# A two-layer fp32 transformer step: first layer begun by chunks, second layer's fold done by transposes and a VectorE sum

## The reference

```python
# layer 0, attention: 16 heads of 8, causal softmax, rms-norm and rope on q and k
qkv = LN(x) @ w_qkv.T;  q, k = rope(rms(q)), rope(rms(k))
x += softmax(causal(q @ k.T / sqrt(8))) @ v @ w_proj.T
# layer 0, mixer: a linear map given in the Fourier domain
x += real(ifft(fft(LN(x)) @ (w_freq_real + 1j * w_freq_imag))) + bias
# layer 1, linear attention: 16 heads of 8, elu + 1 features
x += ((Q @ (K.T @ V)) / (Q @ K.sum()) * sigmoid(stdp)) @ Wo.T + bo
# layer 1, attention over 8 heads of 64; each head's q, k, v is a gated sum of the
# top 3 of 5 experts (gates Ws for q, Wd for k and v), no causal mask;
# the output goes to the experts again by a 0/1 choice and through Wo
x += experts(softmax(q @ k.T / 8) @ v) @ Wo
```

## Time and profile before

| what | value |
|---|---|
| median of 3 runs | 1671.5 us (1671.23 to 1671.99) |
| the profiled execution, its own time | 1671.58 us |
| its span, first to last instruction | 1669.7 us |
| TensorE, VectorE busy | 1553.2 us (93%), 1244.7 us (75%) |
| ScalarE, GpSimd busy | 947.4 us (57%), 825.4 us (49%) |
| mean granted TensorE clock | 0.978 |

### The profile page before, as it was taken

The page is one execution under the profiler, slowest core; times in us unless marked ns, Lnnn a source line. Parts: engine busy times, 40 slices in busy tenths (PEclk is TensorE's granted clock), DMA queues, the critical chain, the costliest instruction groups (busy, mean ns, idle before and its releaser), DMA issues.

```text
span 1669.7 us, 27307 instructions
## 1 busy us (share of the span) xinstructions
PE 1553.2 (93%) x8490; PEld 1012.1 (61%) x8490; DVE 1244.7 (75%) x2525; ACT 947.4 (57%) x1590; POOL 825.4 (49%) x916
## 2 busy tenths in 40 slices
PE   3699999999899997679999999999999999999998
PEld 2455565565566556547667666567576676666565
DVE  3997687688588637787777778787778787777764
ACT  3446756755755662335655655655645656556653
POOL 2530000000001123468758879788689699698552
PEclk9799999999999999889999999999999999999999
DMA  2000000000000000000000000000000000000000
GB/s 64 0 1 1 2 1 1 1 1 1 1 1 1 1 13 12 1 1 13 1 13 1 1 13 1 1 13 1 13 1 1 13 1 1 1 1 1 1 7 20
DMA packets 12231, 9.41 MB, mean 6 GB/s; under 512 B 3840, under 2 KB 11584, under 8 KB 12096
## 3 DMA queue, kind: packets, MB, share of 16 engines
q1 hardware_dynamic: 12096, 7.66, 1.7%
HBM read 6.61 MB, written 1.05 MB: 5 GB/s over the span
## 4 chain that ended last, share of the span: by engine, by line
PE 63%; POOL 17%; DVE 11%; issue 4%; ACT 4%; SPq 1%; DMA 0%; DVEq 0%; ACTq 0%; POOLq 0%
PE ps L920 10%; PE ps L719 8%; PE ps L753 8%; PE ps L738 7%; PE ps L891 5%; PE ps L908 5%; PE ps L678 4%; PE ps L909 4%; POOL gs L1602 4%; POOL gsum L1603 3%; POOL z L583 3%; POOL onm L577 3%; PE ps L931 2%; DVE mxp L1269 2%; POOL h_qk L1604 2%
## 5 line engine op out<-in xcount | busy, mean ns | idle before, releaser
L1148 ACT ACTIVATE pbuf<-ps 128x512 f32<-128x512 f32 x512 | 301.7, 600 | 167.0 <-PE ps L909 163.3
L1013 ACT ACTIVATE pbuf<-ps 128x1024 f32<-128x1024 f32 (+3 forms) x320 | 280.5, 897 | 179.7 <-PE ps L741 91.5
L1269 DVE TENSOR_REDUCE mxp<-ps 128x1 f32<-128x512 f32 (+2 forms) x432 | 278.9, 685 | 88.9 <-PE ps L719 52.0
L1485 DVE TENSOR_TENSOR den<-den,pbuf 128x1024 f32<-128x1024 f32 x224 | 309.9, 1384 | 1.9
L920 PE MATMUL ps<-pbuf,h_v 128*64 128x512 f32 x1024 | 248.0, 605 | 0.0
L1134 ACT ACTIVATE relu<-ps 128x512 f32<-128x512 f32 x256 | 152.2, 598 | 160.2 <-PE ps L891 128.2
L1437 DVE TENSOR_TENSOR gt<-ps,gate 128x320 f32<-128x320 f32 x384 | 181.7, 484 | 77.5 <-POOL h_v L1612 38.8
L719 PE MATMUL ps<-kM,qT 128*128 128x512 f32 (+3 forms) x640 | 230.8, 412 | 8.7 <-ACT kM L1000 4.6
L908 PE MATMUL ps<-q1T,k1T 128*128 128x512 f32 x512 | 215.2, 420 | 10.3 <-ACT pbuf L1148 8.9
L1458 DVE CUSTOM_DVE_ANT_0 relu<-ps,relu 128x512 f32<-128x512 f32 x256 | 174.4, 684 | 67.3 <-PE ps L891 62.5
L738 PE MATMUL ps<-qT,kM 128*128 128x512 f32 (+3 forms) x640 | 202.0, 384 | 8.4 <-ACT pbuf L1013 8.3
(11 more groups left out here) (230 smaller groups left out, 2707.8 us busy)
## 6 DMA issues: line engine op xcount, KB each, us to landing
wraw<-in_Wkv SPq DMA_DIRECT2D x16, 160.0 KB, 2.6
wraw<-in_Wq SPq DMA_DIRECT2D x8, 160.0 KB, 2.2
out<-x SPq DMA_DIRECT2D x4, 256.0 KB, 2.3
wqkv<-in_wqkvT SPq DMA_DIRECT2D x1, 192.0 KB, 4.0
masks<-in_masks SPq DMA_DIRECT2D x1, 128.0 KB, 4.0
dft<-in_dft SPq DMA_DIRECT2D x1, 128.0 KB, 2.3
wout<-in_Wo SPq DMA_DIRECT2D x2, 64.0 KB, 2.6
ident<-in_ident SPq DMA_DIRECT2D x1, 64.0 KB, 5.8
```

What stands on the lines that cost most here:

```text
L1013: nc.scalar.activation(pbuf0[:, u % NP0, :, off:CH], ps[:, b:b + 2, off:CH], ACT.Exp, scale=float(D0) ** -0.5).then_inc(s_exp, 1)
L1148: nc.scalar.activation(pbuf1[:, u % NP1, i, :], ps[:, i, :], ACT.Exp, scale=float(D1) ** -0.5).then_inc(s_exp1, 1)
L1269: v.tensor_reduce(mxp[:, i, h:h + n, b], sc.rearrange("p (h k) -> p h k", h=n), AX.X, ALU.max).then_inc(s_read0d, 1)
L1485: v.tensor_tensor(dn, dn, w, ALU.add).then_inc(s_den1, 1)
```

## The change

1. **Loads.** `x` comes in four DMAs, one a chunk, with a semaphore each; `ident` after the first, `wqkv` after the second, each with its own semaphore. `fold` and its load go.
2. **Start by chunks.** Statistics, root, normalising, transposes, projections and evictions are interleaved by chunk; constants are prepared after the normalising.
3. **First four heads in two halves of 8 tiles.** Squares, roots, rotation and both stagings are done half by half, ahead of `SEQ0`; the first k and q steps wait for their half alone.
4. **Rest.** ScalarE squares the other twelve heads (two ACTIVATEs), GpSimd sums them by pairwise adds; VectorE keeps the reciprocals, now in chunk 1 of group 0. The Fourier matrices move into `SEQ0` (`fq`), the exponent of `stdp` too.
5. **Keeping TensorE at work.** 30 transposes without use ahead of `SEQ0` ("proj") and 40 within chunk 0 ("keys").
6. **Key copies.** Of `kM` for chunks 0 and 1 of groups 1 to 3, two of four copies go to VectorE (`K_BY_DVE`); the step k of chunk 1 comes behind q of chunk 0.
7. **Fold.** `F` is four transposes of `oT`, and VectorE adds the halves by a TENSOR_REDUCE from PSUM; a new step `den` with a bank of its own does the four matmuls for the sums, and VectorE takes the reciprocals and multiplies `on` in SBUF.
8. **q2 of layer 1.** `sq2` is fp32r, and four fp32r matmuls against `identr` replace the four fp32 transposes.

```diff
@@ preparation0
-        out += [(("stagek", g), 3), (("k", g, 0), 1), (("k", g, 1), 1)]
+        out += [(("stagek", g), 3), (("k", g, 0), 1)]
         if late:
             out.append((late, 1))
-        out += [(("stageq", g), 3), (("q", g, 0), 1)]
-        if g == 0:
-            out += [(("rest", 0), 1), (("rest", 1), 1)]
+        out += [(("stageq", g), 3), (("q", g, 0), 1), (("k", g, 1), 1)]
...
+            if (g, c) == (0, 0):
+                items.insert(2, (("fq", 0), 1))
+                items[3:3] = [(("keep", "keys"), 1), (("k", 0, 2), 1), (("rest", 0), 1)]
+                items.insert(9, (("fq", 1), 1))
+            if (g, c) == (0, 1):
+                items.insert(2, (("rest", 1), 1))
@@ foreground1
-                seq.append(("F", (u - 3) // M1 - 1))
+                seq += [("F", (u - 3) // M1 - 1), ("den", (u - 3) // M1 - 1)]
@@ sync
-            sp.dma_start(x[:], A["x"].rearrange("(n p) d -> p n d", p=P)).then_inc(s_load, 16)
+            for c in range(NC):
+                sp.dma_start(x[:, TPC * c:TPC * (c + 1), :], x_v[:, TPC * c:TPC * (c + 1), :]).then_inc(s_x[c], 16)
...
@@ tensor
+            pe.wait_ge(s_ident, 16)
+            transposes1(0)
+            pe.wait_ge(s_wqkv, 16)
+            for n in range(NT):
+                project(n)
+                if n % TPC == 1 and n // TPC + 1 < NC:
+                    transposes1(n // TPC + 1)
             pe.wait_ge(s_qkvev, NT)
             pe.wait_ge(s_const, 1)
...
+            keep_clock(ACC, "proj")
...
@@ q2 of layer 1
-                    chunk_transposes(ring1, step, lambda i: sq2[:, i, 0:D1 + 1], D1 + 1).then_inc(s_turn1, 1)
+                    for i in range(TPC):
+                        mm = pe.matmul(ps[0:D1 + 1, bank, P * i:P * (i + 1)], sq2[:, i, :], identr[:],
+                                       start=True, stop=True)
@@ F of layer 1, tensor
+                    for i in range(TPC):
+                        mm = pe.transpose(ps[:, bank, P * i:P * (i + 1)], oT[:, m % 2, P * i:P * (i + 1)], ident[:])
+                    mm.then_inc(s_turn1, 1)
+                elif kind == "den":
+                    m = step[1]
+                    bank = take(ring1, step)
                     pe.wait_ge(s_den1s, m + 1)
-                    for i in range(TPC):
-                        pe.matmul(ps[:, bank, D1 * i:D1 * (i + 1)], oT[:, m % 2, t], fold[:], ...
...
@@ scalar
+            for n in range(NT):
+                evict(n)
+                if n == 1:
+                    deviations(3)
+                if n % TPC == 1 and n // TPC + 1 < NC:
+                    tokens1(n // TPC + 1)
+                if n == 11:
+                    mean_squares(first, halves[0], 1)
+            act.wait_ge(s_qkvev, NT)
+            for i in range(2):
+                a, _, t, _, _, _ = heads(i, rest, slice(0, NT))
+                nc.scalar.activation(t, a, ACT.Square).then_inc(s_sqr, 1)
+            mean_squares(first, halves[1], 2)
...
-                        for h in range(GH):
+                        for h in range(2 if (g, c) in K_BY_DVE else GH):
@@ vector
+            for k, tiles in enumerate(halves):
+                dve.wait_ge(s_qkvev, NT // 2 * (k + 1))
+                squares(first, tiles)
+                link(roots(first, tiles, k + 1))
+                link(norm_and_rotate(v, link, first, tiles))
+                stage_keys(0, tiles)
+                stage_queries(0, tiles)
...
+                    for h in range(2, GH):
+                        rows = slice(32 * h, 32 * h + 32)
+                        ins = v.tensor_copy(kM[g % 2][rows, h, CH * c:CH * (c + 1)], ps[rows, ring0.bank(step), :])
...
-                    link(v.reciprocal(rd1[:], ps[:, b, TPC * D1:TPC * (D1 + 1)]))
-                    v.tensor_tensor(on[:], ps[:, b, 0:TPC * D1].rearrange("p (n d) -> p n d", n=TPC),
-                                    rd1[:].unsqueeze(2).to_broadcast([P, TPC, D1]), ALU.mult).then_inc(s_read1d, 1)
+                    o = ps[:, ring1.bank(step), :].rearrange("p (n a d) -> p n d a", n=TPC, a=2)
+                    v.tensor_reduce(on[:], o, AX.X, ALU.add).then_inc(s_read1d, 1)
+                elif kind == "den":
+                    m = step[1]
+                    wait_turn(dve, ring1, step)
+                    link(v.reciprocal(rd1[:], ps[:, ring1.bank(step), 0:TPC]))
+                    wait_read(dve, ring1, ("F", m))
+                    v.tensor_tensor(on[:], on[:], rd1[:].unsqueeze(2).to_broadcast([P, TPC, D1]),
+                                    ALU.mult).then_inc(s_read1d, 1)
@@ gpsimd
+            for i in range(2):
+                _, m, t, _, _, _ = heads(i, rest, slice(0, NT))
+                pool.wait_ge(s_sqr, i + 1)
+                link(g_.tensor_tensor(t[:, :, :, 0:4], t[:, :, :, 0:4], t[:, :, :, 4:8], ALU.add))
+                link(g_.tensor_tensor(t[:, :, :, 0:2], t[:, :, :, 0:2], t[:, :, :, 2:4], ALU.add))
+                g_.tensor_tensor(m.unsqueeze(3), t[:, :, :, 0:1], t[:, :, :, 1:2], ALU.add).then_inc(s_msr, 1)
```

More of the change, by code:

```diff
@@ L58 @@
 MAX1 = 2.0
[L59 removed]
+KEEP = {"proj": 30, "keys": 40, "pj": 28, "mix": 20, "lin": 14, "norm2": 8, "norm3": 6, "gates": 16, "end": 18}
 def preparation0():
@@ L179, in merge @@
     return seq
+K_BY_DVE = {(g, c): 2 * (g - 1) + c + 1 for g in range(1, NG) for c in range(2)}
 class Ring:
@@ L331, in build @@
         l1.close()
+        s_x = [sem(f"s_x{c}") for c in range(NC)]
+        s_ident = sem("s_ident")
+        s_sqr = sem("s_sqr")
+        s_msr = sem("s_msr")
+        s_kdve = sem("s_kdve")
+        s_wqkv = sem("s_wqkv")
         s_load = sem("s_load")
@@ L670, in take @@
                 if turn >= len(ring.banks):
-                    wait_read(pe, ring, ring.order[turn - len(ring.banks)])
+                    last = ring.order[turn - len(ring.banks)]
+                    if last[0] == "k":
+                        wait_keys(*last[1:])
+                    else:
+                        wait_read(pe, ring, last)
                 return ring.bank(step)
@@ L1196, in _, with centred @@
             v.memset(ones[:], 1.0)
-            dve.wait_ge(s_load, 16 * 12)
-            statistics(0, NT)
-            dve.wait_ge(s_std, 1)
-            link(v.reciprocal(rstd[:], std[:]))
-            norm(0, NT)
+            def centred(c):
+                tiles = slice(TPC * c, TPC * (c + 1))
+                dve.wait_ge(s_std, c + 1)
+                link(v.reciprocal(rstd[:, tiles], std[:, tiles]))
+                norm(TPC * c, TPC)
+            for c in range(NC):
+                dve.wait_ge(s_x[c], 16)
+                statistics(TPC * c, TPC)
+                if c:
+                    centred(c - 1)
+            centred(NC - 1)
+            dve.wait_ge(s_ident, 16)
+            dve.wait_ge(s_load, 16 * 9)
             v.tensor_copy(identr[:], ident[:])
@@ L1215, in squares @@
                 for i in range(2):
-                    _, m, t, _, _, _ = heads(i, hs)
+                    _, m, t, _, _, _ = heads(i, hs, tiles)
                     ins = v.tensor_reduce(m, t, AX.X, ALU.add)
                 ins.then_inc(s_ms, 1)
-            squares(first)
-            dve.wait_ge(s_rms, 1)
-            for i in range(2):
-                m = heads(i, first)[1]
-                ins = v.reciprocal(m, m)
-            link(ins)
-            link(norm_and_rotate(v, link, first))
@@ L1227, in _, with roots, stage_keys @@
-            dve.wait_ge(s_pconst, 1)
+            def roots(hs, tiles, count):
+                dve.wait_ge(s_rms, count)
+                for i in range(2):
+                    m = heads(i, hs, tiles)[1]
+                    ins = v.reciprocal(m, m)
+                return ins
+            def stage_keys(g, tiles):
+                gk = qkv[:, tiles, D + 32 * g:D + 32 * (g + 1)].rearrange("p n (h d) -> p n h d", d=D0)
+                v.tensor_copy(stagek[:, tiles, :, D0:2 * D0].bitcast(F32R), gk)
+                link(v.tensor_copy(stagek[:, tiles, :, 0:D0].bitcast(F32R), gk))
+                v.tensor_tensor(stagek[:, tiles, :, 2 * D0:3 * D0], gk, stagek[:, tiles, :, 0:D0],
+                                ALU.subtract).then_inc(s_stagek, 1)
```

222 lines of the change are left out of this document (115 added, 107 removed).

## The result

| | before | after |
|---|---|---|
| median, alternating on one chip | 1671.37 us (1669.78 to 1671.99, 4 runs) | 1650.84 us (1649.68 to 1651.37, 4 runs) |
| profiled span | 1669.7 us | 1649.5 us |
| mean granted clock | 0.978 | 0.984 |

The ratio is 0.9878, 95% interval 0.9861 to 0.9895: faster, but by 20.5 us where 45 were forecast, and outside the range of 1609 to 1645.

The account below looks back on a forecast made before the run. The prediction took TensorE, busy 93% of the span, as the main bound, though not everywhere, with GpSimd a third of layer 1's chain. Terms -18 - 14 - 13 = -45 from 1671.5 gave 1626.5 us, range 1609 to 1645.

Parts of the forecast that it names:

- Part 1: The beginning: earlier loads, chunked start and halved heads bring first exponents to about 55.5 us against 73.88, -18 us.
- GpSimd's sums of the other heads run beside it, for which I add 1: Beginning, staging of half 2: GpSimd's sums beside it add 1 us, so it ends at 35.5 instead of 34.5.
- The filling: Chunk 0 of the beginning: 40 idle TensorE transposes take 5.8 us from near 34.5; VectorE idles some 4 us.
- Part 2: Layer 0's three group boundaries: shared key copies nearly remove stalls and half-clock stretches, 4.7 us each, -14 us.
- Part 3: Layer 1's fold and q2: TensorE loses some 20 us of work, of which -13 us counts; bounds -3 and -21.
- two thirds realised: Layer 1: with a third of the chain GpSimd's, two thirds of TensorE's 20 us relief counts, -13 us.
- The 4 us put down for the multiplication beside GpSimd: Layer 1: VectorE's multiplication reading SBUF twice could make GpSimd stand, making the sum 4 us worse by the skill's rule.
- (a): Rival: layer 1 gives nothing, since GpSimd's chain takes back what TensorE is spared; 1639.5 us, chance 0.14.
- (b): Rival: the clock still falls at the group boundaries, as waits for staging remain; 1635.5 us, chance 0.12.
- (c): Rival: all of TensorE's relief counts; 1612.5 us, chance 0.13.
- (d): Rival: TensorE's clock falls once in each of layer 1's 32 chunks, +109 us; 1735.5 us, chance 0.03.
- (e): Rival: in the beginning, idle transposes and ScalarE's longer queue leave only 8 us of gain; 1636.5 us, chance 0.08.

Follow-up runs that it names:

- e3: Changed kernel with GpSimd's clearing of kM0 held back until the four chunks are normalised: 1647.55 us, ratio to before 0.9853.
- e4: Changed kernel with GpSimd's sums of the other twelve heads held back until both halves are staged: 1646.48 us, ratio to before 0.9840.
- e11: Changed kernel with kM0's clearing as GpSimd's first work, small clearings behind the normalising, sums held back, idle transposes kept: 1640.74 us, ratio to before 0.9821.
- e14: e12 with the other heads' root and stdp's exponent moved into chunk 1, VectorE's reciprocals eight steps later in chunk 1: 1637.91 us, ratio to before 0.9796.
- e12: e11 without the 40 idle transposes: 1639.12 us, ratio to before 0.9805; timed again 1640.86 us, ratio 0.9823.
- e5: Changed kernel without the 40 idle transposes of chunk 0: 1647.63 us, ratio to before 0.9850.
- e8: Kernel before with GpSimd's addition into z cut to 8 elements, leaving out most of that sum: 1657.54 us, ratio to before 0.9918.
- e9: Changed kernel with GpSimd's addition into z cut to 8 elements, leaving out most of that sum: 1628.78 us, ratio to before 0.9744.
- e1: Kernel before with only the new F, den step and q2 of layer 1: 1659.44 us beside 1672.01, ratio 0.9926.
- e13: e12 with the other heads' root and stdp's exponent moved into chunk 1, VectorE's reciprocals into chunk 2: 1641.71 us, ratio to before 0.9817.

## Why the prediction was wrong

**The step that failed is Part 1**: "normalised chunks at about 7.2, 9.8, 12.4 and 13.9 us", and behind it "GpSimd's sums of the other heads run beside it, for which I add 1". I took VectorE's durations from a stretch in which GpSimd was idle and moved them to one in which it isn't. The clearing of `kM0` at 4.43, 6.92 us long, is in the trace of before; I did not ask what runs beside the new place of the normalising. In a line:
```profile
4.43 6.92 POOL L1525 MEMSET kM<- 128x8192 f32 x1
```
The runs price the parts of the missing 17 to 18 us (first exponents at 73.1 for 55.5): the clearing 3.3 (e3), or 4.0 between e4 and e11; the sums 4.4 against the 1 I had put in (e4); and the work for the other heads ahead of the first exponents 5.6 to 7.0 there, of which 3.3 to 4.8 last (e14 against the two profiles of e12). I had named the reciprocals' move as a relief; they stood in chunk 1, but still ahead of the first exponents, and the root and the table load on ScalarE stood there too. This last price is the sum of two moves, which no run prices apart. Together this is 12 to 14 us more than I had put in. The filling's 4.5 (e5) is not among them: the 4 us in which VectorE idles were in my 55.5.

That e14 has its first exponents at 55.3 is therefore luck: it has no filling, and with it they would come near 59. Some 3 to 5 of the 18 us stay unexplained by the named causes. The milestones of e11, with both collisions gone and the filling kept, show where they build up: last eviction 24.9 (forecast 22.2), halves staged at 29.4 and 37.6 (26.2 and 35.5), third maximum 45.8 (41).

*The filling* was sized about right, 5.8 us long (measured 5.29) at a price of 4 (4.5), and put at 34.5 (48.53, as all before it was late). TensorE's stream in the changed kernel is nothing but idle transposes from 48.6 to 53.8, right behind the matmuls of `fq`; windows, columns as in the earlier trace rows:
```profile
49.00:50.00 1.00, 1.00 (x6) 1.00 (x5) 0.10 (x1) 0.37 (x1) 0.00 (x0) 0.50 0.00 0
...
51.00:52.00 1.00, 1.00 (x12) 1.00 (x10) 0.00 (x0) 0.00 (x0) 0.00 (x0) 1.00 0.00 0
...
58.00:60.00 2.00, 1.57 (x5) 1.02 (x5) 1.32 (x6) 1.36 (x3) 0.00 (x0) 0.50 0.00 0
```
The granted clock rose from 0.50 to 1.00 within them, and their starts went from 0.21 to 0.11 us apart. Here matmuls ran just before; in the kernel before TensorE had done nothing at all until its 16 transposes from 19.6 us on, and their starts too went from 0.21 us apart (the prediction has 0.19) to 0.11, at 23.07, still within them. The Trainium skill, "TensorE: Matmul & The Clock Gate", section "Part 4: PE-mode transpose", has it that transposes don't raise the clock; the measurement decides. But at 58 us the clock is at 0.50 again. From 54 to 68 us its mean is 0.86, against 0.51 in e5 without the filling, and e5 is ahead by 4.5 us at the first exponents all the same: the filling did keep the clock up for longer, and that was worth less than its length.

**Part 2** was right in mechanism and near in size: 10.8 us of 14, no 0.5 left at the boundaries, the pairs of copies as forecast, 3.6 a boundary instead of 4.7.

**Part 3** had TensorE's relief right (20; e8 and e9 give 19.4), and so the term that was off is "two thirds realised". It was 8.6, or 10.8 without the half-clock stretch, e1 gave 11.7: about half. A share of the chain is no exchange rate: GpSimd's 33% was not a third of each chunk's time but a second chain, which holds back one chunk of every four while the next head's projections run. Three gain 0.4 to 0.7 us and that one loses 0.35 to 0.5, about 0.3 a chunk on the mean; with GpSimd relieved it is 0.6 throughout. The 4 us put down for the multiplication beside GpSimd did not show: GpSimd's multiplications average 1030 ns in both kernels, and VectorE's takes 444 ns for 424.

**The rivals.** (a) named the right mechanism and overdid it: layer 1 gave 8.6, not 0. (b) fell: no profile with the shared copies has a half-clock stretch at a boundary. (c) holds only with GpSimd relieved (e9). (d) fell: one half-clock stretch in 885 us, not 32. (e), at 0.08, had the right place and was still 7 us too good, and its reason, idle transposes and ScalarE's longer queue, leaves out GpSimd's clearing and sums. Each term of the forecast came out smaller than its own value, which my range, built from one rival at a time, did not reach.

## What to carry to other kernels

Before a step of VectorE is moved, read GpSimd's row at its new place: there a duration taken from a quiet stretch need not hold, and even a clearing that reads nothing can stand in the way. When an engine that is no bottleneck lies to a third on the chain, relieve it in an experiment on both kernels: the difference shows what the change is worth without it. A gain in the first microseconds can be lost again where something moves with it: in e13 GpSimd's long rotation landed on a short instruction that others waited for, and 5.4 us went.
